# Second attention of a two-layer decoder: its loop over units taken two at a time

## What is computed

```
ln = layernorm(latents, ln_l_g, ln_l_b)   # latents: LN(x), 1024 a batch
xn = layernorm(ctx, ln_x_g, ln_x_b)       # ctx: 77 a batch
q  = (ln @ Wq)                            # 16 heads of 64
kv = concatenate([xn @ Wkv, ln @ Wkv], axis=1)
...
qn = rmsnorm(q, qn_g) * scale             # over a head's 64 values
kn = rmsnorm(k, kn_g)
sim = einsum('bhid,bhjd->bhij', qn, kn)
sim = where(padded_mask, sim, max_neg)
out = einsum('bhij,bhjd->bhid', softmax(sim), v)
return out @ Wout + bout
```

## Time and profile before

| what | value |
|---|---|
| runs | 2195.23 us median, 2191.35 to 2196.08 |
| profiled execution | 2200.02 us, its span 2198.2 us |
| TensorE busy | 1955.0 us, 89% of the span |
| TensorE weight loads | 1661.2 us, 76% (beside matmuls) |
| VectorE busy | 1254.4 us, 57% |
| ScalarE busy | 1002.8 us, 46% |
| GpSimd busy | 607.8 us, 28% |
| mean granted clock of TensorE | 0.939 |
| second attention, steady stretch 783 to 1508 us | granted clock 1.00 |

### The profile page before, as it was taken

One profiled execution on the slowest core, in us unless ns is written; L12 is line 12 of the kernel. 1 busy time (PEld: TensorE's weight loads), 2 busy tenths in 40 slices (PEclk: granted clock), 3 DMA queues, 4 the chain that ended last, 5 costly groups with the idle time before them and its releaser, 6 DMA issues. The chain is left out here.

```text
span 2198.2 us, 40034 instructions
## 1 busy us (share of the span) xinstructions
PE 1955.0 (89%) x13656; PEld 1661.2 (76%) x13657; DVE 1254.4 (57%) x2963; ACT 1002.8 (46%) x1747; POOL 607.8 (28%) x555
## 2 busy tenths in 40 slices
PE   4888957999579999999999999999999984799994
PEld 2477947999467887787778887877778764799994
DVE  5273064677647766676677676767666656122223
ACT  2543414555245555554555555555555541344441
POOL 2300002333144432442244323432343100222220
PEclk9898958999669999999999999999999995899997
DMA  5501163111322112211221122212211207311113
GB/s 196 172 35 73 62 233 105 47 48 48 110 68 68 42 38 59 68 40 31 68 69 39 39 60 68 49 29 62 69 40 36 56 1 271 125 36 38 33 38 127
DMA packets 93663, 159.24 MB, mean 72 GB/s; under 512 B 22385, under 2 KB 54831, under 8 KB 91707
## 3 DMA queue, kind: packets, MB, share of 16 engines
q1 hardware_dynamic: 82875, 134.32, 21.6%
q0 software_dynamic: 8320, 20.65, 3.1%
q10 hardware_dynamic: 2304, 2.10, 0.3%
HBM read 71.57 MB, written 32.41 MB: 47 GB/s over the span
## 5 line engine op out<-in xcount | busy, mean ns | idle before, releaser
L1873 DVE TENSOR_REDUCE a_part_peak<-a_slot 128x1 f32<-128x512 f32 (+1 forms) x512 | 354.7, 732 | 315.0 <-PE a_slot L1689 314.5
L1832 ACT ACTIVATE a_probT<-a_slot 128x640 f32<-128x640 f32 x256 | 180.4, 705 | 474.8 <-PE a_slot L1698 251.3
L1689 PEld LDWEIGHTS a_slot<-a_KHL,a_QHL 128*128 128x128 f32 x1536 | 271.8, 190 | 121.8 <-issue 53.2
L1689 PE MATMUL a_slot<-a_KHL,a_QHL 128*128 128x512 f32 (+1 forms) x1536 | 343.7, 359 | 22.2 <-DVE a_probT L1896 11.9
L1820 ACT ACTIVATE a_prob<-a_slot,a_npeak 128x1024 f32<-128x1024 f32 x256 | 284.2, 1110 | 3.0 <-DVE a_npeak L1875 3.0
L1714 PE MATMUL a_po<-a_probT,a_V 128*64 128x256 f32 (+1 forms) x2304 | 276.8, 385 | 0.0
L1698 PE MATMUL a_slot<-ident,a_prob 128*128 128x128 f32 x2048 | 266.3, 273 | 0.0
L1698 PEld LDWEIGHTS a_slot<-ident,a_prob 128*128 128x128 f32 x2048 | 235.2, 142 | 8.4
L1714 PEld LDWEIGHTS a_po<-a_probT,a_V 128*64 128x64 f32 (+1 forms) x2304 | 153.6, 136 | 87.0 <-issue 21.5
L1639 PE MATMUL a_side<-a_W,a_latT 128*128 128x128 f32 x1536 | 205.9, 286 | 12.5 <-DVE a_KT L1883 6.6
L1639 PEld LDWEIGHTS a_side<-a_W,a_latT 128*128 128x128 f32 x1536 | 191.9, 201 | 18.8 <-DVE a_KT L1883 11.2
(11 more groups left out here) (319 smaller groups left out, 2989.0 us busy)
## 6 DMA issues: line engine op xcount, KB each, us to landing
a_KHL<-a_KT SPq DMA_DIRECT2D x128, 256.0 KB, 4.6
a_QHL<-a_QT SPq DMA_DIRECT2D x128, 128.0 KB, 2.3
m_up<-_L_ffn_gate_up_proj_dram SPq DMA_DIRECT2D x8, 1024.0 KB, 9.8
m_up<-in_L_ffn_W_dram SPq DMA_DIRECT2D x8, 1024.0 KB, 8.6
m_down<-in_L_ffn_W_dram SPq DMA_DIRECT2D x8, 1024.0 KB, 12.5
a_prob_dram<-a0p_zeros SPq DMA_DIRECT2D x4, 1632.0 KB, 11.0
a_dist_dram<-a_dist SPq DMA_DIRECT2D x4, 1632.0 KB, 8.2
a_band_prob<-a_prob_dram SPq DMA_DIRECT2D x4, 1632.0 KB, 6.8
```

Of the source, the lines that this page charges most:

```text
L1689: ins = t_.matmul(out[:, lo:hi], q, KHL[:, pair.parity, h, part, lo:hi], start=part == 0, stop=part == 1)
L1832: a_.activation(probT[:, u // 4 % 2, HALF:KT_TILES, h, u % 2 * P:(u % 2 + 1) * P], slot[u % 2][:, HALF * P:KT_TILES * P].rearrange("p (t q ...
L1873: v.tensor_reduce(part[:, i:i + 1], slot[u % 2][:, lo:hi], AX.X, ALU.max).then_inc(part_peaked, 1)
```

## The change

The loop over units of a pair goes by two. On TensorE a round is now: turned sums (every second round), transposes of u, a projection, transposes of u + 1, scores of u + 2, scores of u + 3, a FRONT piece, half of a group's weighing, a BEHIND piece. On VectorE: copy of u, the add, copy of u + 1, both row sums, the group's reciprocal and wide copy, both peaks, `bound`, and the subtraction of a FRONT piece. On ScalarE: both copies, exponentials of u + 2, the FRONT piece, exponentials of u + 3, the BEHIND piece. The tables are new, each round has at most one piece ahead and one behind; Ktc comes before the two turned queries, on SyncE's queue too. The prologue makes the exponentials of unit 1 as well as of unit 0.

```diff
-PIECES = ["Ka", "Kb", "c", "Qa", "Qb", "Kta", "V0", "Ktb", "V1", "Qta", "Ktc", "V2", "Qtb", "V3"]
-FRONT = {3: "c", 7: "Kta", 9: "Ktb", 11: "Qta", 13: "Qtb"}
-BEHIND = {0: "Ka", 2: "Kb", 4: "Qa", 6: "Qb", 8: "V0", 10: "V1", 11: "Ktc", 12: "V2", 14: "V3"}
+PIECES = ["Ka", "Kb", "c", "Qa", "Qb", "Kta", "V0", "Ktb", "V1", "Ktc", "Qta", "Qtb", "V2", "V3"]
+FRONT = {0: "Ka", 2: "c", 4: "Qb", 6: "Kta", 8: "Ktb", 10: "Ktc", 12: "Qtb", 14: "V3"}
+BEHIND = {0: "Kb", 2: "Qa", 6: "V0", 8: "V1", 10: "Qta", 12: "V2"}
...
                 spread_keys(pair, "Ktb")
+                spread_keys(pair, "Ktc")
                 spread_queries(pair, 0)
-                spread_keys(pair, "Ktc")
...
-                for u in range(UNITS):
+                for u in range(0, UNITS, 2):
                     one_before, two_before = group_before(pair, u, 1), group_before(pair, u, 2)
-                    if after and u in FRONT:
-                        piece(after, FRONT[u])
                     pe.wait_ge(exped, pair.g * UNITS + (u + 1))
-                    if u % 2 == 1 and two_before[0]:
-                        project_outputs(*two_before, u // 2 % 2)
                     if u % 4 == 2 and one_before[0]:
                         turn_sums(*one_before)
                     turn(pair, u)
-                    if one_before[0] and u % 2 == 1:
+                    pe.wait_ge(exped, pair.g * UNITS + (u + 2))
+                    if two_before[0]:
+                        project_outputs(*two_before, u // 2 % 2)
+                    turn(pair, u + 1)
+                    for k in range(2):
+                        nxt = ahead(pair, u + k, 2)
+                        if nxt[0]:
+                            pe.wait_ge(probT_act, pair.g * UNITS + (u + k + 1))
+                            pe.wait_ge(probT_dve, pair.g * UNITS + (u + k + 1))
+                            score(*nxt)
+                    if after and u in FRONT:
+                        piece(after, FRONT[u])
+                    if one_before[0]:
                         weigh(*one_before, u // 2 % 2)
                     if after and u in BEHIND:
                         piece(after, BEHIND[u])
-                    nxt = ahead(pair, u, 2)
-                    if nxt[0]:
-                        pe.wait_ge(probT_act, pair.g * UNITS + (u + 1))
-                        pe.wait_ge(probT_dve, pair.g * UNITS + (u + 1))
-                        score(*nxt)
...
             exponentials(start, 0)
+            exponentials(start, 1)
...
-                for u in range(UNITS):
+                for u in range(0, UNITS, 2):
+                    copy_rest(pair, u)
+                    copy_rest(pair, u + 1)
+                    first, second = ahead(pair, u, 2), ahead(pair, u, 3)
+                    if first[0]:
+                        exponentials(*first)
                     if after and u in FRONT:
                         piece(after, FRONT[u])
-                    copy_rest(pair, u)
-                    nxt = ahead(pair, u, 1)
-                    if nxt[0]:
-                        exponentials(*nxt)
+                    if second[0]:
+                        exponentials(*second)
                     if after and u in BEHIND:
                         piece(after, BEHIND[u])
...
-                for u in range(UNITS):
+                for u in range(0, UNITS, 2):
...
-                    if after and u in FRONT:
-                        piece(after, FRONT[u])
-                    if u % 2 == 1 and two_before[0]:
...
                     copy_first(pair, u)
+                    if two_before[0]:
...
+                        add_outputs(*two_before, u // 2 % 2)
+                    copy_first(pair, u + 1)
                     row_sum(pair, u)
-                    if u % 4 == 3:
+                    row_sum(pair, u + 1)
+                    if u % 4 == 2:
                         invert(pair, u // 4)
-                    nxt = ahead(pair, u, 2)
-                    if nxt[0]:
-                        peak(*nxt)
-                    if after and u in BEHIND:
-                        piece(after, BEHIND[u])
+                    for k in range(2):
+                        nxt = ahead(pair, u + k, 2)
+                        if nxt[0]:
+                            peak(*nxt)
                     if after and u in BOUND_AT:
                         bound(after, BOUND_AT.index(u))
+                    if after and u in FRONT:
+                        piece(after, FRONT[u])
```

More of the change, by code:

```diff
@@ L1996, in body @@
                     copy_first(pair, u)
+                    if two_before[0]:
+                        if isinstance(pair.g, int) and pair.g == 0 and u == 8:
+                            dve.wait_ge(based, 1)
+                        dve.wait_ge(turned, (pair.g * UNITS + u + 1) * 3 + 1)
+                        add_outputs(*two_before, u // 2 % 2)
+                    copy_first(pair, u + 1)
                     row_sum(pair, u)
-                    if u % 4 == 3:
+                    row_sum(pair, u + 1)
+                    if u % 4 == 2:
                         invert(pair, u // 4)
-                    nxt = ahead(pair, u, 2)
-                    if nxt[0]:
-                        peak(*nxt)
-                    if after and u in BEHIND:
-                        piece(after, BEHIND[u])
+                    for k in range(2):
+                        nxt = ahead(pair, u + k, 2)
+                        if nxt[0]:
+                            peak(*nxt)
                     if after and u in BOUND_AT:
                         bound(after, BOUND_AT.index(u))
+                    if after and u in FRONT:
+                        piece(after, FRONT[u])
             all_pairs(dve, body)
```

## The result

The change is slower: 2241.87 us median (2236.76 to 2242.14, 4 runs) against 2195.65 us (2191.35 to 2197.6, 4 runs), a ratio of 1.0208 with a 95% interval of 1.0187 to 1.0229. I had forecast 2219 us, with 2172 to 2246 as the range. The profiled execution took 2242.01 us, 42.0 us above that of before.

What follows compares the result with a forecast made beforehand. TensorE was taken to set the pace, with 2.5 us of waits in a 72.5 us pair. +36 − 7 − 5 = +24 on 2200.02 gave 2224, less 4.8 for the median 2219 us; range 2172 to 2246.

Steps and rivals of the forecast that it cites:

- rival B: Block 6: GpSimd's scale of K so late that TensorE's Kta transposes wait for it; 2234 us at 1 us; chance 0.15.
- The waits of a pair: TensorE's waits in each pair that prepares a next one: 74.9 against 72.5 us, +2.4, over 15 pairs +36 us.
- the four waits: On TensorE in each pair: V0 waits 3.6 us, V1 0.5, Qta 0.2, V2 0.6, on top of 70.0 us.
- the wait in block 6: V0 on TensorE waits 3.6 us, as GpSimd's scale, square and fold hold VectorE's row sums and wide copy.
- The loop's back edges: Ends of TensorE's loop: 1.2 us won at each of four, −5 us (0 to −9).
- The last pair: Pair without pieces or GpSimd work: two units take 7.3 us instead of 8.24, −7 us (−2 to −9).
- At nothing: Priced at zero: exp(1) in the prologue, key spread ahead of query spread on DMA, earlier adds and normalisations on VectorE.
- C: Row sums get in first and GpSimd waits; V0 waits some 1.9 us, pair 73.2, total 2194 us; chance 0.15.
- A: GpSimd misses the row sums of block 6; pair 71.5 us, total 2168 us; chance 0.22.
- the lock: Block 6: GpSimd's instructions exclude VectorE's row sums and wide copy; a pair costs 71.4 us without it, 74.9 with it.

## Why the prediction came out as it did

The direction and the mechanism of the wait were right, the size was not: +24 us forecast, +42.0 between the two profiled executions (46.2 between the medians). The measured 2241.87 us lies above the forecast's own range of 2200 to 2232; that the whole range holds it is luck, as its upper end was drawn for rival B, which did not happen.

- **The waits of a pair**, +36 us forecast. 75.0 against 72.5 us in pairs at full clock without a loop's end, so 2.5 × 15 = +37.5. In the pair shown each of the four waits came within 0.2 us of its forecast, and the two runs that changed the row sums' place and took away GpSimd's work showed what makes the largest.
- **The step that failed** is the price of the wait in block 6: I put the 3.6 us into the sum at their length and left the granted clock at the 1.00 that the earlier trace rows show. That row is of a loop without idles of this length. The idle also lowered the clock behind it in most pairs: +15 us by the run that filled it, some +20 by the pairs of the change itself. I had no term for that, and no bound.
- **The loop's back edges**, −5 us forecast, came out between 0 (by the ends in the filled run, 2.1 to 2.8 us each) and −3 (by the one end in the change without a fall): 1.3 to 1.45 us of idle remain, and VectorE's end lies beside TensorE's. I had priced one engine alone, and had TensorE's branch go out at its last wait, ahead of V3. It goes out later: at 861.5 us, just behind the start of the last 20 passes of a weighing.
- **The last pair**, −7 us forecast: 8 × (8.24 − 6.9) = −11. I had kept 7.3 us for two units.
- **At nothing**: the first weight load comes 7.6 us earlier, and the first pair is then longer than in before by 5.5 beyond the 2.5 (78.3 us between its loads in the run with the wait filled, 70.3 before), so some −2 us.

By the run that filled the wait 37.5 + 15 + 0 − 11 − 2 = +39.5, by the pairs of the change itself 37.5 + 20 − 3 − 11 − 2 = +41.5, against 42.0. The fifteenth pair's fall of the clock, behind the last weight load, is in neither sum.

Of the rivals, C and B did not happen: it was VectorE's instructions that were long, and Kta waited for nothing. A asked that GpSimd's times shift, and they did not (the scale of K ended 3.76 us into the block, forecast 3.7); the kernel with the peaks between the row sums, which shifts VectorE's instead, went below A's price (2147 against 2168), because its pairs cost 70.4 us without a loop's end where I had 71.5 (of the four waits one of 0.2 us is left, I had kept 1.5 in all), and the last pair gave more. Two slips in the prediction's figures change nothing: a pair without the lock is 71.5 us by its own terms, not 71.4, and a third of C is 0.05, which makes faster 0.27 and slower 0.65.

In the loop of the change all 55 row sums longer than 0.35 us ended 0.09 to 0.10 us behind the end of a GpSimd scale, square, fold or split, and all 14 such wide copies 0.15 us behind the end of a fold; the scale of K itself kept its 2.12 us in all 15 pairs. The Trainium skill (SBUF — State Buffer, section "SBUF: two separate sides") calls the shared port pair an exclusive lock and not a split of bandwidth: whichever starts first has it for its whole instruction, and the other is blocked. The trace agrees in these 69 instances. In the trace of before, 30 row sums ran beside GpSimd's power (3.23 us for the keys, 2.92 for the queries) and took 0.29 us, so not every operation of GpSimd holds VectorE.

A rule that I had not used bears on what I missed: the Trainium skill (TensorE: Matmul & The Clock Gate, section "HAM oscillation — how this bites in real kernels") describes a wait between groups of matmuls that drops the clock each time round. The trace agrees in 11 of the 15 pairs; in the other 4 the clock stayed at 1.00.

## What to carry to other kernels

Where VectorE has short instructions on SBUF and GpSimd long ones, put the short ones behind what the bottleneck waits for, and not in a bunch ahead of it: here three short operations moved behind a peak were worth 4% of the kernel, the clock's part included. A wait that leaves TensorE idle for two to three and a half microseconds in every round can cost more than its length, and here mostly did; price the clock behind it by itself, and look at the granted clock in steps of 1 us before calling it constant. When a back edge is to go, look at every engine that meets in the loop: here TensorE's alone gave 2.7 us, within the noise, and TensorE's, VectorE's and ScalarE's together 9.5.

## What the runs showed of the hardware that I had not expected

- Here the clock fell behind idles: with 14 matmuls by zero added per pair to fill one, the kernel became 15 us faster than the change (12 by the ratios).
- Not every idle of one length has the same effect: 11 of 15 at 3.4 to 3.7 us, 9 of 14 at 2.0 to 2.2, none of those at 1.1 to 1.4 within a pair. At the loop's ends of the runs above, 4 of 20 idles of 1.5 to 2.2 us had a fall behind them.
- With TensorE's loop written out, VectorE stands 2.8 to 3.5 us at each loop's end although its branch instruction itself is short in the trace (0.05 to 0.07 us); on TensorE the taken branch is the long one (3.35 to 3.5 us in the change). Straight code, twice as long, ran without such a wait.
